# Sixteen heads of eight columns: scores from 32 rows of the array in pairs, and keys masked four heads at a time

## What is computed

```python
x = x + tanh(g_xattn[0]) * attention0(layernorm(x), ctx)       # 16 heads of 64
x = x + tanh(g_ffn[0]) * bitlinear_ffn(layernorm(x))
x = x + tanh(g_xattn[1]) * attention1(layernorm(x), ctx, mask) # 16 heads of 8
x = x + tanh(g_ffn[1]) * mixture_of_8_experts(layernorm(x))
x = x + tanh(g_xattn[2]) * attention2(layernorm(x), ctx)       # 1 head of 128
x = x + tanh(g_ffn[2]) * ternary_ffn(layernorm(x))
x = x + tanh(g_xattn[3]) * attention3(layernorm(x), ctx)       # 16 heads of 8
x = x + tanh(g_ffn[3]) * rms_bitlinear_ffn(layernorm(x))

# attention1 and attention3, D_K = 8, NUM_HEADS = 16
scores = einsum('bhqd,bhkd->bhqk', Q, K) / sqrt(8)
scores = where(mask == 0, -1e9, scores)                        # attention1 only
out = einsum('bhqk,bhkd->bhqd', softmax(scores), V)
```

## Time and profile before

| what | value |
|---|---|
| median of three runs | 648.88 us (647.07 to 654.99) |
| span of the profiled execution | 649.0 us |
| TensorE busy | 552.7 us |
| VectorE busy | 378.4 us |
| ScalarE busy | 297.9 us |
| GpSimd busy | 154.5 us |
| mean granted TensorE clock | 0.898 of full |

### The profile page before, as it was taken

The page is one execution under the profiler, slowest core; times in us unless marked ns, Lnnn a source line. Parts: engine busy times, 40 slices in busy tenths (PEclk is TensorE's granted clock), DMA queues, the critical chain, the costliest instruction groups (busy, mean ns, idle before and its releaser), DMA issues.

```text
span 649.0 us, 9365 instructions
## 1 busy us (share of the span) xinstructions
PE 552.7 (85%) x3199; PEld 421.1 (65%) x3213; DVE 378.4 (58%) x1019; ACT 297.9 (46%) x558; POOL 154.5 (24%) x249
## 2 busy tenths in 40 slices
PE   5889899999768887888799999996877999888952
PEld 4578788887756665766556776774554676656731
DVE  1277678777976766776451111114446778687673
ACT  3354355554424442434244334432565665565552
POOL 3060000000333312351100000001324444445242
PEclk9999899999998877998789999997577999898855
DMA  9500000000000000000001111100000000000000
GB/s 365 175 0 2 1 1 2 1 1 2 2 0 2 2 0 1 1 1 1 1 1 33 34 32 63 34 0 0 2 0 1 1 2 1 1 2 0 1 1 32
DMA packets 2715, 12.97 MB, mean 20 GB/s; under 512 B 433, under 2 KB 561, under 8 KB 2418
## 3 DMA queue, kind: packets, MB, share of 16 engines
q1 hardware_dynamic: 2674, 12.44, 5.2%
HBM read 11.91 MB, written 0.52 MB: 19 GB/s over the span
## 4 chain that ended last, share of the span: by engine, by line
PE 62%; DVE 18%; issue 8%; ACT 7%; POOL 3%; DMA 1%; another core or an unknown queue 0%; DVEq 0%; POOLq 0%; ACTq 0%
PE bank L868 9%; PE bank L878 9%; PE bank L721 5%; PE bank L729 5%; PE bank L746 4%; PE bank L763 4%; PE bank L716 4%; PE bank L742 3%; DVE prob L1098 3%; DVE xn L1067 3%; PE bank L758 2%; POOL rstd L419 2%; PE bank L709 2%; PE bank L852 2%; PE bank L697 2%
## 5 line engine op out<-in xcount | busy, mean ns | idle before, releaser
L417 POOL TENSOR_SCALAR rstd<-mv 128x1 f32<-128x1 f32 x64 | 13.2, 206 | 417.6 <-DVE mv L1053 415.7
L1092 DVE TENSOR_REDUCE mx<-bank 128x4 f32<-128x512 f32 x96 | 66.0, 688 | 56.4 <-PE bank L721 38.1
L486 ACT ACTIVATE prob<-prob 128x512 f32<-128x512 f32 x96 | 60.1, 626 | 61.9 <-DVE prob L1098 61.6
L476 ACT ACTIVATE probT<-bank 128x512 f32<-128x512 f32 (+1 forms) x104 | 58.9, 568 | 44.1 <-PE bank L729 43.3
L729 PEld LDWEIGHTS bank<-pack,prob 128*128 128x128 f32 x384 | 50.6, 150 | 37.4 <-issue 26.6
L721 PE MATMUL bank<-kz,qT 128*128 128x512 f32 x128 | 73.9, 662 | 0.1
L586 ACT ACTIVATE kz<-bank,expert 128x512 f32<-128x512 f32 x64 | 44.0, 687 | 61.9 <-PE bank L868 61.8
L1248 DVE SCALAR_TENSOR_TENSOR pack<-bank,w_tok,pack 128x128 f32<-128x128 f32 x64 | 18.0, 344 | 88.5 <-PE bank L878 88.5
L746 PEld LDWEIGHTS bank<-va,probT 128*128 128x128 f32 x512 | 68.6, 208 | 0.7 <-ACT probT L476 0.7
L746 PE MATMUL bank<-va,probT 128*128 128x9 f32 x512 | 66.9, 258 | 0.7 <-ACT probT L476 0.4
L1098 DVE TENSOR_TENSOR prob<-bank,mx 128x512 f32<-128x512 f32 x96 | 65.1, 678 | 2.7 <-PE bank L729 1.8
(11 more groups left out here) (211 smaller groups left out, 929.3 us busy)
## 6 DMA issues: line engine op xcount, KB each, us to landing
expert<-experts_d SPq DMA_DIRECT2D x8, 514.0 KB, 3.3
pack<-pack_d SPq DMA_DIRECT2D x1, 2112.0 KB, 14.7
pack<-pack_d SPq DMA_DIRECT2D x1, 2048.0 KB, 9.7
pack<-pack_d SPq DMA_DIRECT2D x2, 512.0 KB, 11.3
pack<-pack_d SPq DMA_DIRECT2D x1, 973.0 KB, 4.9
mask_i<-mask_d SPq DMA_DIRECT2D x1, 512.0 KB, 16.0
out_d<-pack SPq DMA_DIRECT2D x1, 512.0 KB, 2.7
pack<-pack_d SPq DMA_DIRECT2D x1, 461.5 KB, 10.2
```

Of the source, the lines that this page charges most:

```text
L476: act.activation(dst, src, ACT.Identity if kw else ACT.Copy, **kw).then_inc(E[layer][name].sem, 1)
L486: act.activation(prob[:, g % 2, :], prob[:, g % 2, :], ACT.Exp, scale=float(DK0 if layer == A0 else DK) ** -0.5).then_inc(E[layer]["probs" ...
L1092: yield from do(dve.tensor_reduce(m, src, AX.X, ALU.max))
```

## The change

`kz` now holds 4 copies of the keys, not 16. In copy j the rows of every fourth head remain: rows 8j to 8j + 7 of each of the four blocks of 32 rows. One instruction of 128x512 makes them, in slot 2. Group g's scores are the product of rows 32g to 32g + 31 alone, of queries and keys. The four products lie in four different blocks of rows of the array and use the same 512 columns of `kz`.

The products are given out in pairs: `row_scores` claims both banks, puts in both masks (A1), waits for queries and keys, and issues the products of g and g + 1 one behind the other. Pair 0 stands in slot 0, pair 1 in slot 2 behind `probsT` of group 0; slots 1 and 3 have no scores any more. VectorE's maximum of either group waits until both of its pair are done. A0 keeps its form.

```diff
-            def mask_keys(it, layer, kT, half):
+            def mask_keys(it, layer, kT):
...
-                heads = H // 2
-                pool.tensor_tensor(kz[:, it.k, 1024 * half:1024 * half + 1024].rearrange("p (h t) -> p h t", h=heads),
-                                   kT[:, bass.ds(it.b, 1), :].to_broadcast([P, heads, P]),
...
+                pool.tensor_tensor(kz[:, it.k, 0:GH * P].rearrange("p (h t) -> p h t", h=GH),
+                                   kT[:, bass.ds(it.b, 1), :].to_broadcast([P, GH, P]),
...
-                A1: [[(0, rs, A1)], [(0, mask_keys, A1, kT_1, 0)], [(0, mask_keys, A1, kT_1, 1)], []],
+                A1: [[(0, rs, A1)], [], [(0, mask_keys, A1, kT_1)], []],
...
+            def row_scores(it, layer, pair):
+                for g in (2 * pair, 2 * pair + 1):
+                    claim(it, layer, f"s{g}")
+                    if layer == A1:
+                        add_mask(it, layer, g)
+                if pair == 0:
                     wait(pe, layer, "q_sb", it)
-                    wait(pe, layer, "kz", it, 1 + g // 2)
-                    mm_ = pe.matmul(out[:, :], qT[:, it.k, 0:P], kz[:, it.k, 512 * g:512 * g + 512],
-                                    start=neg is None, stop=True)
-                mm_.then_inc(E[layer]["scores"].sem, 1)
+                    wait(pe, layer, "kz", it)
+                for g in (2 * pair, 2 * pair + 1):
+                    rows = slice(32 * g, 32 * g + 32)
+                    pe.matmul(bank[S_BANK[g % 2]][:, :], qT[rows, it.k, 0:P], kz[rows, it.k, 0:GH * P],
+                              start=layer == A3, stop=True).then_inc(E[layer]["scores"].sem, 1)
...
-                    [(1, scores, layer, 0), (2, probsT, layer, 2), (2, pv, layer, 1), (3, ot, layer)],
...
+                    [(1, row_scores, layer, 0), (2, probsT, layer, 2), (2, pv, layer, 1), (3, ot, layer)],
...
-                wait(dve, layer, "scores", it, g + 1)
+                wait(dve, layer, "scores", it, g + 1 if layer == A0 else 2 * (g // 2) + 2)
```

More of the change, by code:

```diff
@@ L46 @@
 SLOTS = 4
-PACK_FIRST = dict(ctxT=N, wkT_1=P, wkT_3=P, wvT_13=2 * P, ident=P, ones=P, causal=P, hmask=H, bk_3=1, bq_3=1, gates=8, x=N)
+PACK_FIRST = dict(ctxT=N, wkT_1=P, wkT_3=P, wvT_13=2 * P, ident=P, ones=P, causal=P, hmask=GH, bk_3=1, bq_3=1, gates=8, x=N)
 PACK_ATT0 = dict(wkT_0=H * DK0, wqT_0=H * DK0, wvT_0=H * DK0, woT_0=H * DK0)
@@ L308, in build @@
             F0: events(F0, **ffn, gate=1, up=1, tanh=1, gate_sb=1, up_sb=1, quant=5, hid=7),
-            A1: events(A1, **att, q=1, q_sb=1, kz=2, norm=2, ot=1, ot_sb=1),
+            A1: events(A1, **att, q=1, q_sb=1, kz=1, norm=2, ot=1, ot_sb=1),
             ROUTE: events(ROUTE, ln=3, rs=2, xt=1, xt_sb=1, copied=1, logits=1, lg=2),
@@ L314, in build @@
             F2: events(F2, **ffn, up=1, gelu=1, hid=3, rs_hid=2),
-            A3: events(A3, **att, q=1, q_sb=1, kz=2, norm=2, ot=1, ot_sb=1),
+            A3: events(A3, **att, q=1, q_sb=1, kz=1, norm=2, ot=1, ot_sb=1),
             F3: events(F3, **ffn, quant=8, rq=2, up=1, relu=1, squared=1, biased=1, sumsq=1, hw=1, rh=2, hq=7),
@@ L439, in weigh @@
                 pool.tensor_tensor(hid2[:, it.k, :], hid[:, it.k, :], col["nw2"], ALU.mult).then_inc(E[F3]["hw"].sem, 1)
-            def mask_keys(it, layer, kT, half):
-                if it.rep == 0 and half == 0:
+            def mask_keys(it, layer, kT):
+                if it.rep == 0:
                     pool.wait_ge(kv_act, 2 if layer == A1 else 6)
@@ L448, in mask_keys @@
                     wait(pool, A0, "scores", Item(B - 2 + it.k, B - 2 + it.k))
-                heads = H // 2
-                pool.tensor_tensor(kz[:, it.k, 1024 * half:1024 * half + 1024].rearrange("p (h t) -> p h t", h=heads),
-                                   kT[:, bass.ds(it.b, 1), :].to_broadcast([P, heads, P]),
-                                   col["hmask"][:, heads * half:heads * half + heads].rearrange(
-                                       "p (h a) -> p h a", a=1).to_broadcast([P, heads, P]),
+                pool.tensor_tensor(kz[:, it.k, 0:GH * P].rearrange("p (h t) -> p h t", h=GH),
+                                   kT[:, bass.ds(it.b, 1), :].to_broadcast([P, GH, P]),
+                                   col["hmask"].rearrange("p (h a) -> p h a", a=1).to_broadcast([P, GH, P]),
                                    ALU.mult).then_inc(E[layer]["kz"].sem, 1)
@@ L466, in _ @@
                 F2: [[(0, rs, F2)], [], [(1, rs_hid)], []],
-                A3: [[(0, rs, A3)], [(0, mask_keys, A3, kT_3, 0)], [(0, mask_keys, A3, kT_3, 1)], []],
+                A3: [[(0, rs, A3)], [], [(0, mask_keys, A3, kT_3)], []],
                 F3: [[(0, rs, F3)], [(0, rms, "quant", 1, qs, P, "rq")], [(1, weigh), (1, rms, "sumsq", 1, hs, F, "rh")], []],
@@ L697, in xt, with add_mask @@
                 pe.transpose(bank[R_BANK[0]][:, 0:P], src[:, it.k, :], ident).then_inc(E[layer]["xt"].sem, 1)
+            def add_mask(it, layer, g):
+                neg = neg0 if layer == A0 else neg1
+                if g == 0 and it.rep == 0:
+                    if layer == A0:
+                        pe.wait_ge(prep_dve, 2)
+                    pe.wait_ge(pool_const, 2 if layer == A0 else 5)
+                pe.matmul(bank[S_BANK[g % 2]][:, :].rearrange("p (h t) -> p h t", h=GH), identb[:, :],
+                          neg[:, bass.ds(it.b, 1), :].to_broadcast([P, GH, P]), start=True, stop=False)
             def scores(it, layer, g):
@@ L702, in scores @@
                 out = bank[S_BANK[g % 2]]
[L703 to L718, removed]
-                    wait(pe, layer, "q_sb", it)
-                    wait(pe, layer, "kz", it, 1 + g // 2)
-                    mm_ = pe.matmul(out[:, :], qT[:, it.k, 0:P], kz[:, it.k, 512 * g:512 * g + 512],
-                                    start=neg is None, stop=True)
@@ L723, in scores @@
-                mm_.then_inc(E[layer]["scores"].sem, 1)
+                add_mask(it, layer, g)
+                wait(pe, A0, "q_sb", it, 1 + g // 2)
+                wait(pe, A0, "k_sb", it, 2 + 2 * (g // 2))
+                for c in range(2):
+                    t = 2 * g + c
+                    mm_ = pe.matmul(out[:, 256 * c:256 * c + 256], qT[:, it.k, P * t:P * t + P],
+                                    kz[:, it.k, 256 * t:256 * t + 256], start=False, stop=(c == 1))
+                mm_.then_inc(E[layer]["scores"].sem, 1)
@@ new lines, in row_scores @@
+            def row_scores(it, layer, pair):
+                for g in (2 * pair, 2 * pair + 1):
+                    claim(it, layer, f"s{g}")
+                    if layer == A1:
+                        add_mask(it, layer, g)
+                if pair == 0:
+                    wait(pe, layer, "q_sb", it)
+                    wait(pe, layer, "kz", it)
[3 more added lines that the diff above has]
+                              start=layer == A3, stop=True).then_inc(E[layer]["scores"].sem, 1)
@@ L959, in attention @@
                 return [
-                    [(1, scores, layer, 0), (2, probsT, layer, 2), (2, pv, layer, 1), (3, ot, layer)],
-                    [(1, scores, layer, 1), (2, probsT, layer, 3), (2, pv, layer, 2), (3, y, layer)],
-                    [(1, scores, layer, 2), (1, probsT, layer, 0), (2, pv, layer, 3), (0, xt, layer)],
-                    [(1, scores, layer, 3), (1, probsT, layer, 1), (0, q, layer), (1, pv, layer, 0)]]
+                    [(1, row_scores, layer, 0), (2, probsT, layer, 2), (2, pv, layer, 1), (3, ot, layer)],
+                    [(2, probsT, layer, 3), (2, pv, layer, 2), (3, y, layer)],
+                    [(1, probsT, layer, 0), (1, row_scores, layer, 1), (2, pv, layer, 3), (0, xt, layer)],
+                    [(1, probsT, layer, 1), (0, q, layer), (1, pv, layer, 0)]]
             stages = {
@@ L1004, in note @@
             def note(layer, fn, it, *args):
-                if fn not in (route_places, kv3):
+                if fn is row_scores:
+                    order.extend((layer, f"s{g}", it.rep) for g in (2 * args[1], 2 * args[1] + 1))
+                elif fn not in (route_places, kv3):
                     order.append((layer, piece_name(layer, fn, (it, *args)[1:]), it.rep))
@@ L1414 @@
         ident=np.eye(P, dtype=f), ones=np.ones((P, P), f),
-        hmask=(part[:, None] // DK == np.arange(H)[None]).astype(f),
+        hmask=(part[:, None] // DK % GH == np.arange(GH)[None]).astype(f),
         bk_3=a["L3_xattn_b_k"], bq_3=a["L3_xattn_b_q"],
```

## The result

The changed kernel takes 715.7 us (median of 4 runs, 712.72 to 720.62) where the kernel before takes 649.88 us. That is a factor of 1.10, 95% interval 1.095 to 1.108: 66 us slower, where 23 us faster was forecast. Here is the page of the changed kernel: busy time by engine, the granted clock in 40 slices, the chain by engine, and three of its groups.

A forecast was written before the change was run, and what follows sets the result against it. No engine was saturated; A1 was a chain with holes, A3 bound by TensorE, then VectorE. From 649.0 us, less 10.5 (A1 early), 5.5 (half clock), 2.2 (A1 later) and 5 (A3): 625.8, so 626 us; range 606 to 643.

The forecast's parts named there:

- The masking, and VectorE's blocked time: GpSimd's 16 maskings, 0.98 us each, would block VectorE's layer norm line L1067 for 10 us in place of 37.
- The scores on TensorE: A pair of score products would partly overlap on TensorE: 1.29 us plus 0.37 for form changes, against 1.72 before.
- The first rival: A pair's two score products run wholly side by side, 0.43 us less for each of 32 pairs: 615 us, chance 0.18.
- the 0.37 us for changes: Cost on TensorE of changing the array's form to and fro for each pair, taken from 0.33 to 0.4 us.
- I count TensorE's work as unchanged: TensorE's score pairs at 1.66 against 1.72 us, 2 us less over 32 pairs, treated as no change in its work.
- The rival of the low clock: TensorE's holes go but clock drops remain, so the 5.5 + 1 + 1 us fall away: 633 us, chance 0.16.
- The half clock of A1 as a gain of 5.5 us: In A1's early steps beside F0, shorter holes would remove two thirds of TensorE's clock drops: 5.5 us gained.
- The pair as a new wait: VectorE waits for both products of a pair; A1's later step of 13.1 us becomes 12.7, keeping 0.4 of 2.3 gained.
- The rival that priced it: The lost second bank decides: VectorE waits 2.3 us per pair, 73 us against 38.1; 657 or 667 us, chance 0.07.
- The prediction's sign for a dearer wait: A3's steps beside F3 taking over 15 us would show the pair's wait to be dearer than reckoned.

## Why the prediction was wrong

The ledger, by medians: 650 to 616 us by the masking; to 678 by the pairs on full rows; to 716 by taking 32 rows, where the overlap's gain and the clock's price are both inside. Or the other way: 616 to 784 by 32 rows one at a time, and back to 716 by pairing them. At half clock a single product on 32 rows takes 2.07 us and a whole pair 2.08, so 32 pairs should save 66 us; measured are 68.

- *The masking, and VectorE's blocked time:* right. An instruction takes 1.04 us (16.7 us over 16) where 0.98 was taken. `xn` means 407 ns where 0.5 us was said. In A1's later steps it gives 2.2 us of the 2.3, and by itself 32 to 34 us, more than the 23 of the whole forecast. A1's early steps took 61.7 / 4 = 15.4 us at 0.97 with it, as the prediction wanted (15 to 17 us above 0.93); in the changed kernel they took 19.3 at 0.68.
- *"The scores on TensorE", 1.29 us a pair:* wrong, on the good side. 1.13 us with the drain is 0.97 without, against 0.86 for two wholly side by side. The first rival had this step right. My reason against it, the order of the instructions, fell: the first starts of both products lie 0.01 us apart. From the pair's start to that of the next product 1.06 us pass, the change of form behind it included, so the 0.37 us for changes were rather too much.
- *"I count TensorE's work as unchanged":* this is the first step that failed. It counts instructions and durations at the clock of before. With the scores on 32 rows TensorE stood at half clock for most of both layers while it was almost never idle: in the changed kernel 123.7 of 129.7 us busy at 0.50 from 219.2 us to 348.9, 131.6 of 134.8 at 0.50 from 529.9 us to the last scores; one at a time 69.3 of 69.3 us in three steps. All its products there take longer, so the unchanged count became 89 us more of busy time. The rival of the low clock looked at gaps (5.5 + 1 + 1 us) and could not see it. No row of before had a long product on fewer than 128 rows, and I gave that no bound.
- *The half clock of A1 as a gain of 5.5 us:* the mechanism was right where full products remained. With the small masking A1's early steps have 0.97 where 0.85 stood.
- *"The pair as a new wait":* the second step that failed, in size. I had it cost 1.9 us in a later step of A1, the same beside F2, and 1 us beside F3, and nothing in the five steps beside F0, where VectorE has other work. Measured on full rows: 62 us for 16 items, some 4 us an item, lower clock included. The rival that priced it, 73 us of VectorE's wait against 38.1, was right in the wait (79.8) and near in time for that part alone (657, or 667 with its half clock, against 678). It had a chance of 0.07: its reason against was the 2 to 3 us of other work beside F0, and I followed one late step, where the pair's wait almost fitted, and carried it to the others. The prediction's sign for a dearer wait, steps beside F3 of over 15 us, came with 19.5; but half clock lengthens them too, so it does not tell the two failures apart.
- *The range,* 606 to 643, held neither: both failures lie on one side and add up. That the run with query blocks took 625.5 us, the forecast's 626, is chance: it has neither the overlap nor the pair's wait.

## What to carry to other kernels

Before moving long products to part of the array's rows, ask what will keep TensorE's clock up: here the overlap saved its time, and 32 rows cost more than it gave; full rows with zeros in them kept the clock up. Two banks filled together are not two buffers; price a pair in every kind of step, not only in the one where it fits. And when a change has two halves, a masking and a form of product, each belongs in its own run: the masking alone, or with blocks on the query side, was worth 4 to 5% (the masking alone leaves a part of the computation out, the query blocks do not).

## What the runs showed of the hardware

- TensorE can stand at half clock without a gap in its work: 56.4 of 56.4 us busy at 0.50 with 32 rows in pairs, 32.7 of 32.7 us at 1.00 with 128 rows. The Trainium skill ("TensorE: Matmul & The Clock Gate", Part 1) says that the clock follows how busy TensorE has been. If busy means the busy time of the profile, this case disagrees. Whether a product covers all rows counts in some way, and busy time in the profile does not show it. Which rule the chip follows was not measured. Zeros as such are not it: the query blocks are zero in 96 of 128 rows and kept 0.919.
- Two float32 products on different blocks of 32 rows, into different banks, take little more than the time of one: 1.13 against 1.02 us at full clock, 2.08 against 2.07 at half. The Trainium skill ("TensorE: Matmul & The Clock Gate", Part 3) says that such products start a few ns apart, and the trace agrees, with 0.01 us or less.
- A change of the array's form is cheap beside this: some 13 us for two changes and a small product at each of 64 groups, at a clock of 0.930.
